# Two LoRA layers with residuals on one core: V's seven products summed in PSUM in another order, the operand sums on VectorE, and the rank correction in fp32r

## The reference

```python
# layer 0, adapter chosen by label0[b]; LORA_SCALING = 0.5
x = x + (x @ W0.T + (x @ A0[label0]) @ B0w.T * 0.5)
# layer 1, adapter chosen by slot1[b]; SCALING = 2
x = x + (x @ W1.T + bias + (x @ A1[slot1]) @ B1[slot1] * 2)
```

## Time and profile before

| what | us |
|---|---|
| median of 3 runs | 330.48 (328.05 to 331.49) |
| the profiled execution | 328.25 |
| its span | 326.4 |
| mean granted clock of TensorE | 0.979 |
| TensorE busy | 303.4 |
| VectorE busy | 238.5 |
| ScalarE busy | 138.1 |
| GpSimd busy | 101.4 |

### The profile page before, as it was taken

The page is one execution under the profiler, slowest core; times in us unless marked ns, Lnnn a source line. Parts: engine busy times, 40 slices in busy tenths (PEclk is TensorE's granted clock), DMA queues, the critical chain, the costliest instruction groups (busy, mean ns, idle before and its releaser), DMA issues.

```text
span 326.4 us, 4343 instructions
## 1 busy us (share of the span) xinstructions
PE 303.4 (93%) x1397; PEld 247.0 (76%) x1397; DVE 238.5 (73%) x308; ACT 138.1 (42%) x219; POOL 101.4 (31%) x94
## 2 busy tenths in 40 slices
PE   7997988759999999299999999999999999999995
PEld 5886766648788888187887878878878878878874
DVE  2437699979939999986587598587687687677321
ACT  4574364529242475524424424424434525435110
POOL 4426197990110060007007007026025033042000
PEclk9999999969999999879999999999999999999999
DMA  6996700800004400017318227336246255203002
GB/s 200 333 293 135 166 4 0 130 0 0 2 9 65 67 14 0 1 28 143 112 31 166 87 45 156 88 54 152 75 71 154 56 87 138 56 0 129 0 25 104
DMA packets 99361, 27.55 MB, mean 84 GB/s; under 512 B 84885, under 2 KB 93077, under 8 KB 99350
## 3 DMA queue, kind: packets, MB, share of 16 engines
q1 hardware_dynamic: 99350, 27.41, 36.1%
HBM read 19.01 MB, written 8.39 MB: 84 GB/s over the span
## 4 chain that ended last, share of the span: by engine, by line
PE 81%; DVE 11%; issue 3%; ACT 2%; DMA 1%; POOL 1%; SPq 0%; DVEq 0%; ACTq 0%
PE bank L939 79%; DVE s_lo L632 3%; PE bank L953 2%; DVE t_lo L632 2%; DVE a_lo L717 1%; DMA a<-in_L_cond_W 1%; DVE m L632 1%; DVE a1d L632 1%; DVE b_lo L632 1%; DVE v_lo L632 1%; DVE a_lo L632 1%; DVE t L632 1%; POOL b_st L346 0%; ACT b L436 0%; DVE p_lo L632 0%
## 5 line engine op out<-in xcount | busy, mean ns | idle before, releaser
L939 PE MATMUL bank<-vt_hi,s_hi 128*128 128x512 f32 x96 | 37.7, 393 | 0.0
L939 PE MATMUL bank<-vt_lo,s_hi 128*128 128x512 f32 x96 | 37.7, 393 | 0.0
L939 PE MATMUL bank<-vt_hi,s_lo 128*128 128x512 f32 x96 | 37.5, 390 | 0.0
L783 DVE STREAM_TRANSPOSE xt<-raw 128x512 int32<-128x512 int32 x32 | 32.0, 1080 | 0.0
L396 POOL TENSOR_TENSOR s_sum<-xt 128x512 f32<-128x512 f32 x16 | 23.8, 1490 | 20.3 <-PE bank L939 19.6
L632 DVE TENSOR_TENSOR s_lo<-s_sum,s_hi 128x512 fp32r<-128x512 f32 x32 | 27.6, 883 | 3.4 <-ACT s_hi L436 3.4
L388 POOL CAST ac<-c_hi 128x128 fp32r (+1 forms) x8 | 2.3, 291 | 87.9 <-PE bank L939 86.5
L436 ACT ACTIVATE lhs_hi<-xt 128x512 fp32r<-128x512 f32 x32 | 19.9, 628 | 22.5 <-PE bank L939 17.8
L939 PE MATMUL bank<-t_hi,s_hi 128*128 128x512 f32 x48 | 20.0, 417 | 8.6 <-DVE s_lo L632 8.6
L632 DVE TENSOR_TENSOR lhs_lo<-xt,lhs_hi 128x512 fp32r<-128x512 f32 x32 | 24.1, 759 | 4.9 <-ACT lhs_hi L436 4.6
L436 ACT ACTIVATE s_hi<-s_sum 128x512 fp32r<-128x512 f32 x32 | 19.8, 629 | 16.3 <-PE bank L939 9.2
(11 more groups left out here) (165 smaller groups left out, 774.8 us busy)
## 6 DMA issues: line engine op xcount, KB each, us to landing
raw<-in_x SPq DMA_DIRECT2D x32, 256.0 KB, 4.8
out<-y SPq DMA_DIRECT2D x32, 256.0 KB, 2.1
n<-in_L_cond_W SPq DMA_DIRECT2D x16, 256.0 KB, 5.2
a<-in_L_cond_W SPq DMA_DIRECT2D x16, 256.0 KB, 5.3
a_raw<-in_L_cond_lora_A SPq DMA_DIRECT2D x8, 128.0 KB, 2.4
a_raw<-in_L_cond_lora_As SPq DMA_DIRECT2D x8, 64.0 KB, 2.4
b_raw<-in_L_cond_lora_Bs SPq DMA_DIRECT2D x8, 64.0 KB, 2.0
b_raw<-in_L_cond_lora_B_w SPq DMA_DIRECT2D x1, 128.0 KB, 6.1
```

The costliest lines, as they stand in the source:

```text
L783: nc.vector.transpose(xt[:, n, :, :].rearrange("p e (s sb) -> p sb e s", sb=GR).bitcast(I32), rows[:, n // 2, n % 2].bitcast(I32)).then_in ...
L939: return nc.tensor.matmul(ps, lhsT, rhs, start=start, stop=stop, skip_group_check=more)
```

## The change

V's seven products come in the order m1 m7 m6 m2 m3 m5 m4, and PSUM accumulates across them. m7 is added on m1 in `LOW` (copied out as `m17`), m6 on that (copied as `ym`), m5 on that, which is v22. m2 opens `HIGH`: v11 = m2 + m1 is a sum on VectorE, and m3 is accumulated on m2. So `vt2` = m2 + m3 + m17, `vt3` = vt2 - v11, `vt1` = v22 - vt2, `v21` = m4 + ym and `vt4` = v21 - vt2 are VectorE's, and `w` is gone. m7 and m6 stay by halves (`by_halves`). m1 is by k with the high and the low part of a11 apart (`vm1_high`, `vm1_low`), with the turns of b22 and b12 among them on three turning banks instead of two; b21 is turned within m6. The loads go n11/a11, n22, n12, b0, a21 (n22, n12 and a21 by halves), a22, n21, a12, then the a1 slots. The sums s1 to s4, t4 and batch 0's sums of x move from GpSimd to VectorE. x is loaded after the first q.

In the batches `corr` is in fp32r: `b0a1` is held as high and low parts in 48 columns (zeros ahead of column 32), against all 128 rows of `u_st`, in two matmuls of 256 columns. So the first 32 rows of u are split before the correction (`u0_hi_made`, `u0_lo_made`), rows 32 to 47 after it. The product b0 a1 of the V stage is eight matmuls of 256 columns with the parts of a1 side by side (`a1_st`) instead of sixteen of 128.

The cut diff (the tiles' places, and parallel lines, are left out):

```diff
-        M1, M2, M7, M6, M3, M5, M4 = range(0, 7 * HK, HK)
+        M1, M7, M6, M2, M3, M5, M4 = range(0, 7 * HK, HK)
...
-        TURN_BANK = [bank[6], bank[7]]
-        Q_BANK = [bank[5], bank[3]]
+        HIGH = [bank[5], bank[4], bank[7], bank[6]]
+        TURN_BANK = [bank[6], bank[7], bank[4]]
+        Q_BANK = [bank[5], bank[6]]
...
+            for h in range(2):
+                for j in range(2 * h, 2 * h + 2):
+                    load_n(n22, 1, 1, j, n22_in[h])
+                for j in range(2 * h, 2 * h + 2):
+                    load_n(n12, 1, 0, j, n12_in[h])
+                if h == 0:
+                    sp.dma_start(b0_raw[:, 0:KT, :], b0w.rearrange("(t p) r -> p t r", p=P)).then_inc(b0_in, 16)
+                for j in range(2 * h, 2 * h + 2):
+                    load_a(a21, 1, 0, j, a21_in[h])
+            for j in range(HK):
+                load_a(a22, 1, 1, j, a22_in[j // 2])
             for j in range(HK):
                 load_n(n21, 0, 1, j, n21_in[j])
+            for j in range(HK):
                 load_a(a12, 0, 1, j, a12_in[j])
...
-            sp.wait_ge(v_done, M7 + HK)
+            sp.wait_ge(q_done, 1)
             load_x(0)
...
-                tt(s3[:, PAIR[h], :], a21[:, PAIR[h], :], a11[:, PAIR[h], :], ALU.subtract, s3_made)
...
-                tt(s4[:, PAIR[h], :], s2[:, PAIR[h], :], a12[:, PAIR[h], :], ALU.subtract, s4_made)
...
+            s3_sum(0)
+            t3_sum(0)
+            t3_sum(1)
+            t1_sum(0)
+            t1_sum(1)
+            b0_low()
+            s3_low(0)
             t3_low(0)
-            s3_low(0)
-            q_half(0)
+            s3_sum(1)
+            t3_sum(2)
+            t3_sum(3)
+            s3_low(1)
             t3_low(1)
-            s3_low(1)
-            for m in range(HK):
-                v11_low(m)
+            for h in range(2):
+                if h == 1:
+                    t1_sum(2)
+                    t1_sum(3)
+                t2_sum(h)
+                s1_sum(h)
+                s2_sum(h)
+                t2_low(h)
+                s2_low(h)
...
+            def vt23(m):
+                dve.wait_ge(v_done, M3 + m + 1)
+                dve.wait_ge(vm17_made, m + 1)
+                tt(vt2[:, m, :], HIGH[m][:, :], m17[:, m, :], ALU.add, vt2_made)
+                dve.wait_ge(vt2_made, m + 1)
+                dve.wait_ge(v11_lo_made, m + 1)
+                tt(vt3[:, m, :], vt2[:, m, :], v11[:, m, :], ALU.subtract, vt3_made)
...
+            def v22_vt1(m):
+                dve.wait_ge(v22_hi_made, m + 1)
+                tt(v22_lo[:, m, :], LOW[m][:, :], v22_hi[:, m, :].bitcast(F32), ALU.subtract, v22_lo_made)
+                tt(vt1[:, m, :], LOW[m][:, :], vt2[:, m, :], ALU.subtract, vt1_made)
...
-            warm_up(9)
+            warm_up(11)
             turn_b11(0)
-            warm_up(4)
+            warm_up(7)
+            vm1_high(0)
             turn_b11(1)
-            vm1(0)
+            vm1_low(0)
+            vm1_high(1)
             turn_b11(2)
-            vm1(1)
             turn_b11(3)
-            vm1(2)
-            turn_b21(0)
-            vm1(3)
...
+            vm1_low(1)
+            vm1_high(2)
             turn_b22(0)
             turn_b22(1)
-            vm2(2)
+            vm1_low(2)
+            turn_b12(0)
+            turn_b12(1)
+            vm1_high(3)
             turn_b22(2)
             turn_b22(3)
...
+            vm1_low(3)
...
+                for m in range(HK):
+                    if h == 0:
+                        pe.wait_ge(vm1_made, m + 1)
+                    by_halves(h, S3, T3, m, v_done)
             for h in range(2):
                 pe.wait_ge(vs_lo_made, S2_AT + h + 1)
                 pe.wait_ge(t_lo_made, T2_AT + h + 1)
-                for m in (range(HK) if h else (2, 3, 0, 1)):
+                for m in range(HK):
                     if h == 0:
...
+                        pe.wait_ge(vm17_made, m + 1)
+                    by_halves(h, S2, T2, m, v_done)
+                    if h == 1 and m == 2:
+                        turn_b21(HK - 1)
...
+            for k in range(KT):
+                last = mm(B0A1_BANK[:, 0:2 * G1], b0_st[:, k, :],
+                          a1_st[:, k, :, :].rearrange("p part g -> p (part g)"), k == 0, k == KT - 1)
...
+                row_product(HIGH[m], A12, B21, m, True, v_done)
+            pe.wait_ge(vs_lo_made, S4_AT + 2)
+            for m in range(HK):
+                pe.wait_ge(v11_made, m + 1)
+                row_product(HIGH[m], S4, B22, m, False, v_done)
...
             def corr():
-                mm(BANK_E[32:UB, 0:S], b0a1[:, :], u_sum[0:R0, :], True, True).then_inc(corr_done, 1)
+                mm(BANK_E[0:UB, 0:S], b0a1[:, 0, :], u_st[:, :], True, False)
+                mm(BANK_E[0:UB, 0:S], b0a1[:, 1, :], u_st[:, :], False, True).then_inc(corr_done, 1)
...
                 pe.wait_ge(m1_made, b + 1)
-                pe.wait_ge(u_sum_made, b + 1)
+                pe.wait_ge(u0_lo_made, b + 1)
```

More of the change, by code:

```diff
@@ L80, in two_layer_lora_kernel @@
[L80 to L91, removed]
@@ L439, in high, with bank_copy, a11_high @@
                 copy(tile[:, part, :], of[:, part, :], made)
-            for j in range(HK):
-                act.wait_ge(turned, j + 1)
-                copy(b11_hi[:, j, :], TURN_BANK[j % 2][:, :], w1_hi_made)
+            def bank_copy(tile, m, ps, made):
+                copy(tile[:, m, :], ps[:, :], made)
+            def a11_high(j):
                 act.wait_ge(a11_in[j], 16)
@@ L670, in _ @@
[L670 to L678 removed]
+            b11_low(0)
@@ L831, in _ @@
-            a0_low(0)
-            for g in range(3):
-                a_low(0, g)
+                tt(u_st[96:64 + UB, :], u_sum[32:UB, :], u_st[32:UB, :].bitcast(F32), ALU.subtract, u_lo_made)
+            for g in range(4):
+                a_low(0, g)
+            for h in range(2):
+                dve.wait_ge(c_hi_made, h + 1)
+                tt(c_lo[:, HK * h:HK * h + HK, :], CT_BANK[h][:, :].rearrange("p (t n) -> p t n", t=HK),
+                   c_hi[:, HK * h:HK * h + HK, :].bitcast(F32), ALU.subtract, c_lo_made)
@@ L879, in batch @@
             def batch(b, first, final):
-                a_low(b, 3)
-                b1_low(b)
+                if not first:
+                    a_low(b, 3)
+                    b1_low(b)
                 dve.wait_ge(m6_done, b + 1)
@@ L903, in batch @@
                 tt(z_sum[:, :], BANK_C[:, :], u2_sum[:, :], ALU.add, z_made)
-                if not final:
+                if first:
+                    turn_next(b + 1, range(2, 3))
+                    h_sum(b)
+                elif not final:
                     a_low(b + 1, 2)
@@ L908, in batch @@
                 tt(z_sum[:, :], BANK_D[:, :], z_sum[:, :], ALU.add, z2_made)
-                h_and_low(b)
+                if not first:
+                    h_sum(b)
+                u_low(b)
+                if first:
+                    turn_next(b + 1, range(3, 4))
+                    a_low(b + 1, 0)
+                    a0_low(b + 1)
+                    a_low(b + 1, 2)
                 if not final:
@@ L1065, in _ @@
                 q_step(Q_BANK[0], j, B11, j, j == 0, False)
-            for j in range(HK):
-                last = q_step(Q_BANK[0], HK + j, B21, j, False, j == HK - 1)
-            last.then_inc(q_done, 1)
+            turn_b12(2)
+            turn_b12(3)
             for h in range(2):
@@ new lines, in _ @@
+                if h == 0:
+                    for j in range(HK - 1):
+                        turn_b21(j)
+            for j in range(HK):
+                pe.wait_ge(w1_lo_made, HK + j + 1)
+                last = q_step(Q_BANK[0], HK + j, B21, j, False, j == HK - 1)
+            last.then_inc(q_done, 1)
+            pe.wait_ge(a1_lo_made, 1)
+            pe.wait_ge(w1_made, 3 * HK)
+            c_first(0, A11)
+            pe.wait_ge(w0_lo_made, 2 * HK)
+            c_first(1, A12).then_inc(ct_done, 1)
```

754 lines of the change are left out of this document (394 added, 360 removed).

## The result

The changed kernel takes 300.65 us (median of 4 runs, 300.59 to 300.90), the kernel before 330.64 beside it (4 runs, 328.05 to 331.49). The ratio is 0.911, 95% interval [0.906, 0.916]. The forecast was 302.0 us, with a range of 298.5 to 311.

A forecast was written before the change was run, and what follows sets the result against it. TensorE, busy for 303.4 of 326.4 us, was taken as the bound. Terms of 26.8 us left a span of 299.6; 1.85 around it gave 301.5, and half a microsecond for the median 302.0 us, range 298.5 to 311.

The forecast's parts named there:

- the terms of the sum: Savings priced over the whole profiled execution, from start to corrections: 26.8 us together, taking the span from 326.4 to 299.6.
- Waits in V (8.6 + 2.0): V stage: TensorE's waits for VectorE's low parts of S (8.6 us) and ScalarE's bank copies (2.0) would go.
- the start: Before V's first matmul: warm-ups and transposes end at 6.8 instead of 7.23; gain .6 us, bounds 0 and .9.
- The price of a 128x1024 operation, 1.14: VectorE's sums and subtractions: 1.14 us each at best, 3.4 at worst; 1.14 taken, the row without GpSimd sums.
- The walk: Check along the new TensorE list that each operand is made before it is due; V-stage margins of 1 to 2 us.
- an early wait stays: Rival: V-stage margins fail, 2 to 4 us waited, 2.4 at half clock if long; 304 to 308 us, chance .23.
- The walk to batch 0: V stage's due times: S3's first half at 24.4, batch 0 starting at 110.6, its `u_product` due at 116.1.
- Batch 0's wait, 6.4, and half clock, 1.6 + .5: Before batch 0's `u_product`: the 6.4 us wait, on `a_low(0, 3)`, goes, and the 1.6 + .5 at half clock after it.
- Batch 0's own length: Batch 0, from its `u_product` to the next: no long wait, clock 1.00, a batch of 23.06 us.
- The walk's closest place: Batch 0's low-rank product: operand there at 126.5 against 126.0 due.
- Correction, .49 a batch, 3.9: `corr` in each of 8 batches: .73 us in fp32 becomes .24 in fp32r; 3.9 in all, bounds 0 and 5.8.
- b0 a1, .8: V stage's product b0 a1: sixteen matmuls (1.7 us) become eight (.96); gain .8, bounds 0 and 1.

The follow-up runs named there:

- b_dve_sums: The kernel before with the ten 128x1024 operand sums (s3, s1, s2, s4, t4) on VectorE instead of GpSimd: 321.90 us, ratio 0.977.
- a_pool_tt: The changed kernel with five 128x1024 GpSimd sums that nobody reads added behind a22's diagonals: 311.75 us, ratio 0.947.
- a_pool_memset: The changed kernel with fourteen 128x1024 GpSimd memsets added behind a22's diagonals: 301.42 us, ratio 0.915.
- a_old_loads: The changed kernel with the loads in the old order: 311.56 us, ratio 0.946.
- b_both: The kernel before with the ten operand sums on VectorE, batch 0's fourth quarter of x split early and batch 0's VectorE list rearranged: 318.39 us, ratio 0.969.
- b_quarter4: The kernel before with only the split of batch 0's fourth quarter of x moved behind the first three: 329.48 us, ratio 0.999.
- third group: One of three groups of follow-up runs, each with its own runs of the kernel before; here their median was 328.43 us (17 runs).
- a_y_early: The changed kernel with C12's output sum in batch 0 ahead of a low part of the next batch: 300.59 us, ratio 0.914.
- b_filler: The kernel before with 50 and 54 idle transposes on TensorE in its two long waits: 328.96 us, ratio 0.996.
- b_q4_list: The kernel before with batch 0's fourth quarter of x split early and batch 0's VectorE list rearranged as in the changed kernel: 325.65 us, ratio 0.990.

## Why the prediction came out right

The median was 1.35 us under the forecast, the profiled execution .8 (300.67 against 301.5). The mechanism held, but the closeness is in part luck. Up to batch 0's `u_product` the terms of the sum give 137.75 - 20.8 = 116.95, and it was 115.14, 1.8 us less; batch 0 then took 1.1 more than the terms give (25.75 - 2.1 - .49 = 23.16, it was 24.22), and the rest came out as summed.

- *Waits in V (8.6 + 2.0).* Right. None over .5 us after 6.4. The cause of the longest, VectorE's operations beside GpSimd's sums, is shown from both sides: b_dve_sums brings the 6.17 down to 1.88, a_pool_tt brings one of 7.2 back, a_pool_memset doesn't. That it also needs the loads is shown by a_old_loads, 10.9 us. The 2.0 for ScalarE's copies stand in b_dve_sums and b_both as before; no run takes them away by themselves. The sum took the idle times as shown, and a wait costs more than that: the one of 1.37 at 49.94 cost 1.64, as the matmuls from 48.18 over 49.94 to 50.28 are 2.10 apart in place of .45. With .2 more at the start and a wait of .3 for m that the sum put at nothing, such margins at four or five waits make, by my estimate, most of the 1.8.
- *The price of a 128x1024 operation, 1.14.* It was 1.21 to 1.23, 7% more. The walk had rounded the other way elsewhere: s_lo and t_lo of S3's first half ended at 22.9 (walk 23.3), S2's first half at 33.8 (33.65), its second at 41.0 (40.6), where 42.3 was due. Each spare held, so the rival *an early wait stays* (.23) fell.
- *The walk to batch 0.* S3 began at 24.26 against 24.4, `u_product` at 115.14 against 116.1. The start gave .4 more (6.40, where I took 6.8), the V stage the rest.
- *Batch 0's wait, 6.4, and half clock, 1.6 + .5.* Both gone, clock 1.00. b_quarter4 shows that the cause named was the right one, but that removing it was not sufficient: without the other edits 2.0 of it stay. The prediction gave these edits no term of their own, since its walk was of the whole list; had it priced the parts singly it would have been wrong.
- *Batch 0's own length was mis-sized.* It took for granted a batch of 23.06 and got 24.22, 1.2 more. Nearly all of it is at the two places with a wait: from start to start of the matmuls around them, they cost .35 and .57 beyond the usual .227, and the next matmul .1 each. VectorE is full and beside GpSimd's sums there (four operations of 1.5 to 1.8). The walk's closest place, the low-rank product with 126.0 against 126.5, is where .20 was waited: its operand came about as walked, TensorE 1.0 us earlier. So the 1.0 that V gained on the walk was lost again in batch 0.
- *Correction, .49 a batch, 3.9.* 23.55 to 23.06 is .49 in a steady batch; taking it back costs 3.5 us of the median, since batch 0 hardly gains by it. The Trainium skill (FP8 and Floating Point Precision, TensorE Precision Notes) gives true FP32 four passes; with one for fp32r, which is my reading of that section, the estimate was .24 a batch. The row was the better guide.
- *b0 a1, .8.* Not taken out by itself, but the trace has it: the eight matmuls run from 55.24 to the next product at 56.19, .95 us where the walk had .96 and the sixteen of before took 1.7.

```profile
55.24 1.11 PE L1096 MATMUL bank<-a_st,b_st 128*128 128x256 f32 x8
```

From the two ends together: of 27.8 us in the third group (328.43 to 300.59), b_both has 10.0 (VectorE's sums and batch 0's list) and the correction 3.5. The 14.3 left belong to the two orders, of V's products and of the loads, with b0 a1 (.8) and the start (.8). The 10.9 of a_old_loads is not the loads' share of these: it is what the new order of V loses when the loads come in the old one. How the 14.3 divide stays open, since neither order was run alone in the kernel before. The figures come from three groups, whose medians of the kernel before differ by up to 1.4 us.

## What to carry to other kernels

Walk the whole list of the engine that feeds the bound, operand by operand with its due time, rather than price edits singly: a wait that is removed alone passes its time to the next operand of the same list (of 6.4 us, 2.0 were kept). Elementwise work on GpSimd that reads SBUF is not free beside VectorE's two-input operations: one of the two is held up, by 2.1 us for a 128x1024 operation of VectorE here (1.2 became 3.3). Fp32 in one small product of a loop can cost several times what its column count says (.73 us, where an fp32r matmul of the same columns takes .12).

## What the runs showed of the hardware that I had not expected

- Either side can be the one held up. Beside VectorE's unbroken list two of GpSimd's eight casts of c's high part (128x128) took 2.75 and 2.46 us in the changed kernel; the other six took .29, as all eight did before. In the kernel before, two sums of GpSimd took 10.38 us while VectorE's two-input operations in that time kept their 1.2 each. What decides which side waits was not tested.

```profile
117.28 2.46 POOL L385 CAST ac<-c_hi 128x128 fp32r<-128x128 f32 x1
...
62.88 10.38 POOL L325 TENSOR_TENSOR s<-s,a 128x1024 f32<-128x1024 f32 x2
...
63.39 2.34 DVE L632 TENSOR_TENSOR t_lo<-t,t_hi 128x1024 fp32r<-128x1024 f32 x2
```

- The kernel before spreads over 4.3 us between executions (327.63 to 331.96 in 19 runs), the changed one over .3 (300.59 to 300.90 in 4), and a_y_early too (300.33 to 300.64 in 6). The kernels with long waits spread by .6 to 5.4 us. Why was not tested, but the traces have a lead. In the profiled executions of b_filler and b_q4_list, whose lists are those of the kernel before up to there, VectorE reaches S3's low parts 1.8 to 1.9 us later, one of them runs beside GpSimd's sum, and S3 starts at 46.57 and 47.98 instead of 42.83. The kernel before, then b_filler:

```profile
41.30 1.48 DVE L632 TENSOR_TENSOR s_lo<-s,s_hi 128x1024 fp32r<-128x1024 f32 x1
...
43.12 3.39 DVE L633 TENSOR_TENSOR s_lo<-s,s_hi 128x1024 fp32r<-128x1024 f32 x1
```

- A gain in one execution's profile (b_quarter4: 2.0 us of span) can be missing in the medians of ten; the profiled execution was the fastest of these ten. An expectation should be set against medians where the kernel spreads by more than the gain.
